# The order of SyncE's transfers in a projection's last batch, and a feed-forward stage and a long convolution put into one program

## The reference

```python
x = x + jnp.tanh(g_xattn[0]) * _L0_xattn_ref(_layernorm(x, axis=-1), ctx_2048, mask, mask, Wq, bq, Wk, bk, Wv, bv)
x = x + jnp.tanh(g_ffn[0]) * _L0_ffn_ref(_layernorm(x, axis=-1), w_gate, w_up, w_down)
x = x + jnp.tanh(g_xattn[1]) * _L1_xattn_ref(_layernorm(x, axis=-1), k, fside, ctx_2048, ctx_2048, 8)
x = x + jnp.tanh(g_ffn[1]) * _L1_ffn_ref(_layernorm(x, axis=-1), w_fc, w_proj)
```

```python
kv = vr[:, :, :, None, :] * x2r[:, :, None, :, :]      # all 64 pairs (i, j) of a group
y = causal_convolution(kv, k[group]) + kv * skip
out = jnp.einsum('bhijl,bhil->bhjl', y, x1r)
```

## Time and profile before

| | |
|---|---|
| median of 3 runs | 1246.86 us (1246.72 to 1247.12) |
| profiled execution | 1245.74 us, of which the span from the first to the last instruction is 1243.9 |
| TensorE (PE) busy | 1075.5 us, 86% |
| VectorE (DVE) busy | 997.0 us, 80% |
| ScalarE (ACT) busy | 695.9 us, 56% |
| GpSimd (POOL) busy | 514.3 us, 41% |
| mean granted TensorE clock | 0.953 of full speed |

### The profile page before, as it was taken

The page is one execution under the profiler, slowest core; times in us unless marked ns, Lnnn a source line. Parts: engine busy times, 40 slices in busy tenths (PEclk is TensorE's granted clock), DMA queues, the critical chain, the costliest instruction groups (busy, mean ns, idle before and its releaser), DMA issues. The chain is left out here.

```text
span 1243.9 us, 14018 instructions
## 1 busy us (share of the span) xinstructions
PE 1075.5 (86%) x4802; PEld 421.4 (34%) x4802; DVE 997.0 (80%) x1521; ACT 695.9 (56%) x835; POOL 514.3 (41%) x403
## 2 busy tenths in 40 slices
PE   4889689999999999778999967999999996279586
PEld 2444222222222222134444433444444443134232
DVE  4368679999999996298999955888788878677897
ACT  2777488888888888746666641110000000786996
POOL 2665323553543543611011017878887881000111
PEclk9999899999999999999999988999999997599889
DMA  9899733644644642051111110112212120000011
GB/s 325 268 380 385 241 114 104 194 128 136 192 125 135 197 123 92 28 195 51 35 52 35 52 38 29 57 52 68 68 51 68 52 67 1 0 1 1 18 51 68
DMA packets 73703, 132.89 MB, mean 107 GB/s; under 512 B 18336, under 2 KB 37152, under 8 KB 73120
## 3 DMA queue, kind: packets, MB, share of 16 engines
q1 hardware_dynamic: 73632, 132.00, 32.5%
HBM read 107.58 MB, written 22.02 MB: 104 GB/s over the span
## 5 line engine op out<-in xcount | busy, mean ns | idle before, releaser
L897 DVE TENSOR_REDUCE mneg<-ps_m 128x1 f32<-128x512 f32 x512 | 326.4, 685 | 40.0 <-PE ps_m L809 36.3
L1470 PE MATMUL ps_y<-kv,toeplitz_sb 128*128 128x512 f32 x640 | 279.1, 595 | 8.8 <-POOL kv L1382 8.8
L749 ACT ACTIVATE probs<-ps_s 128x1024 f32<-128x1024 f32 x256 | 250.7, 1022 | 37.9 <-PE ps_s L842 37.8
L1470 PEld LDWEIGHTS ps_y<-kv,toeplitz_sb 128*128 128x128 f32 x640 | 120.9, 191 | 154.8 <-issue 154.8
L842 PE MATMUL ps_s<-qk_stack 128*128 128x512 bf16 x512 | 139.6, 387 | 29.2 <-ACT probs L749 28.2
L852 PE MATMUL ps_o<-probs,v_all 128*17 128x512 f32 x1024 | 135.8, 603 | 0.0
L1382 POOL TENSOR_TENSOR kv<-vT,ctxT_sb 128x2048 f32<-128x2048 f32 x32 | 118.7, 3711 | 39.2 <-PE ps_y L1470 32.1
L1088 PE MATMUL ps_g<-w,xT_f 128*128 128x512 bf16 x512 | 119.6, 382 | 11.5 <-DVE h_f L1254 7.9
L809 PE MATMUL ps_m<-qk_stack 64*128 64x512 bf16 x512 | 112.1, 392 | 15.2 <-DVE mneg L897 8.1
L1435 ACT ACTIVATE w_anchor<-w_f 128x512 f32<-128x512 f32 x32 | 20.1, 628 | 180.6 <-DMA w_f<-in_w 180.6
L1536 DVE TENSOR_TENSOR z<-ps_y,ctxT_sb 128x1024 f32<-128x1024 f32 x64 | 77.9, 1218 | 46.8 <-PE ps_y L1470 46.8
(11 more groups left out here) (163 smaller groups left out, 1613.7 us busy)
## 6 DMA issues: line engine op xcount, KB each, us to landing
qk_stack<-qk_parts SPq DMA_DIRECT2D x192, 128.0 KB, 2.9
w_sweep<-in_w SPq DMA_DIRECT2D x8, 1536.0 KB, 11.8
qk_parts<-qk_part SPq DMA_DIRECT2D x16, 768.0 KB, 9.0
w_sweep<-in_w SPq DMA_DIRECT2D x16, 768.0 KB, 5.5
w_sweep<-in_w SPq DMA_DIRECT2D x16, 512.0 KB, 3.6
toeplitz_sb<-in_toeplitz SPq DMA_DIRECT2D x32, 256.0 KB, 2.6
w_f<-in_w SPq DMA_DIRECT2D x32, 256.0 KB, 2.9
v_rows<-vp SPq DMA_DIRECT2D x8, 544.0 KB, 10.0
```

The lines of the kernel that those rows point to most:

```text
L749: nc.scalar.activation(pr[:, k % 2, 2 * slot:2 * slot + 2, :], S[:, 2 * slot:2 * slot + 2, :], ACT.Exp).then_inc(exp_done, 1)
L897: nc.vector.tensor_reduce(mneg[:, h, tc, hd:hd + 1], M[:, bank_, :], AX.X, ALU.max, negate=True).then_inc(max_red, 1)
L1470: mm = nc.tensor.matmul(Y[:, q % 3, l2, :], T[:, g % 2, (lt - m) * P:(lt - m + 1) * P], kv[:, g % 2, m, :], start=(m == 0), stop=(m == lt))
```

## The change

Two parts.

SyncE's order. `load_constants` is split from `load_masks`. In the last batch, after the store of the key parts, SyncE now issues the weights of unit 0, then the masks and the three leading blocks of slot 2, then stores query parts and values, then everything else (other blocks and constants of slot 2, weights of unit 1, all of slot 3). The wait of `evacuate` in unit 0 is split: the even sums wait for the values of even batches, the odd ones for those of odd batches.

One program. Feed-forward and the convolution are issued in one block. Feed-forward's tiles work in the order of `ORDER`: first the 8 row blocks of channels 0-127 (t even), then the others. Their normalisation factors are made on their own: `ln_variance` in tile 9, `ln_scalar` on ScalarE in tile 9, `ln_inverse` and a shift in tile 10. ScalarE normalises the 8 row blocks in tiles 12 to 15 (`normalise_ahead`, two a tile) directly into the part of vT that is free; TensorE turns them at the end of feed-forward (`turn_in`, two before the down product of tile 14, six after it, before tile 15's hidden values are turned) and ScalarE places them. GpSimd goes on with the partition reduction and the first products after tile 14's update; tile 15's update comes after the first products. The other 8 row blocks are turned in during groups 2 to 9. Tensors of the convolution are laid over those of feed-forward, and waits guard that.

```diff
-LN_COLUMNS = ((0, ROWT), (0, ROWT - 2), (ROWT - 2, ROWT), (0, ROWT), (0, ROWT))
+LN_COLUMNS = (range(ROWT), range(ROWT - 2), range(ROWT - 2, ROWT), range(0, ROWT, CT), range(1, ROWT, CT), range(ROWT))
+ORDER = (*range(0, ROWT, CT), *range(1, ROWT, CT))
...
         if h == 0:
-            sp.wait_ge(wsum_ready, 3 * B)
-            load_unit(core, sp, 1, 0)
-        else:
             sp.wait_ge(k_done, B)
             sp.wait_ge(v_done, B)
             load_weights(sp, 0, 0)
-            sp.wait_ge(f_ready, 2 * B)
-            load_unit(core, sp, 1, 1)
+            sp.wait_ge(wsum_ready, 3 * B)
+            load_masks(core, sp, 1, 0)
+            load_blocks(core, sp, 1, 0, range(LEAD))
+        else:
+            load_blocks(core, sp, 1, 0, range(LEAD, BLOCKS))
+            load_constants(core, sp, 1, 0)
             load_weights(sp, 1, 1)
+            load_masks(core, sp, 1, 1)
+            load_blocks(core, sp, 1, 1, range(BLOCKS))
+            load_constants(core, sp, 1, 1)
...
-            if u == 0 and G == 0:
-                for p in range(2):
-                    act.wait_ge(v_stored[p], 16 * (B // 2))
+            if u == 0:
+                act.wait_ge(v_stored[G], 16 * (B // 2))
...
             if last:
+                pe.wait_ge(h_ready, NCH * ROWT - 1)
+                for i in range(2):
+                    turn_in(pe, i)
                 down(t - 1, 1 - par, False)
+                for i in range(2, ROWT // 2):
+                    turn_in(pe, i)
                 turn_h(t, par, False)
                 down(t, par, False)
...
+                if c == 3 and t == ROWT // 2 + 1:
+                    ln_scalar(core, act, 3)
+                if c in (1, 3) and t >= ROWT - 4:
+                    normalise(act, 2 * (t - ROWT + 4) + c // 2)
             if last:
+                for i in range(2):
+                    place(act, i)
                 take_down(t - 1, 1 - par, False)
+                for i in range(2, 4):
+                    place(act, i)
                 round_h(t, par)
+                for i in range(4, ROWT // 2):
+                    place(act, i)
                 copy_h(t, par)
                 take_down(t, par, False)
...
+                if c == 2 and t == ROWT // 2 + 2:
+                    ln_inverse(core, dve, 3)
+                    nc.vector.scalar_tensor_tensor(core.x_shift[:, 0:ROWT:CT], core.mean[:, 0:ROWT:CT], -1.0,
+                                                   core.rstd[:, 0:ROWT:CT], ALU.mult, ALU.mult)\
+                        .then_inc(shift_ready, 1)
...
+                if c == 3 and t == ROWT // 2 + 1:
+                    ln_variance(core, dve, 3)
...
+    def normalise_ahead(act, b):
+
+        if b == 0:
+            act.wait_ge(shift_ready, 1)
+        t = CT * b
+        nc.scalar.activation(rows(b), X[:, t, :].rearrange("p (l c) -> p l c", l=LT), ACT.Identity,
+                             bias=core.x_shift[:, t:t + 1], scale=core.rstd[:, t:t + 1]).then_inc(xe_ready, 1)
...
+    def gpsimd(pool):
+        pool.wait_ge(w8_run, ROWT)
+        nc.gpsimd.partition_all_reduce(w8s[:, MA, :], core.w8_max, P, bass.bass_isa.ReduceOp.max)\
+            .then_inc(w8_all, 1)
...
+            if g % (NGRP // 2) == 0:
+                pool.wait_ge(vT_ready, ROWT if g else HALF)
+            if g == 0:
+                pool.wait_ge(h_ready, NCH * ROWT)
...
+        for g in range(NGRP):
+            products(g)
+            gains(g)
+            if g == 0:
+                ffn_update(pool, ROWT - 1)
...
+        for g in range(NGRP):
+            pe.wait_ge(T_loaded[g % 2], 16 * (g // 2) + 16)
+            pe.wait_ge(kv_ready, g + 1)
+            if g == 1:
+                pe.wait_ge(d_taken, ROWT)
+            convolve(g, 0)
+            convolve(g, 1)
+            if 2 <= g < HALF + 2:
+                turn_in(pe, HALF + g - 2)
...
+            if g == 0:
+                ffn_statistics(dve, ROWT - 1)
+                ln_variance(core, dve, 4)
+            if g == 1:
+                ln_inverse(core, dve, 4)
```

More of the change, by code:

```diff
@@ L70, in load_masks, with load_constants @@
                          src[:, b].unsqueeze(1).to_broadcast([HD, QUAD, L])).then_inc(core.qk_lead[slot], 16)
-            if b < 2:
-                sp.dma_start(heads[SIDE * (1 - a) + LEAD:SIDE * (2 - a):STEP],
-                             src[BLOCKS:BLOCKS + 1, 0].unsqueeze(1).to_broadcast([HD, QUAD, L]))\
-                    .then_inc(core.qk_rest[slot], 16)
+def load_constants(core, sp, b, h):
+    slot = 2 * (b % 2) + h
+    for a in range(2):
+        for dst, src in ((core.Q, core.mask_q), (core.K, core.mask_k)):
+            sp.dma_start(dst[slot][SIDE * (1 - a) + LEAD:SIDE * (2 - a):STEP, QUAD * a:QUAD * (a + 1), :],
+                         src[BLOCKS:BLOCKS + 1, 0].unsqueeze(1).to_broadcast([HD, QUAD, L]))\
+                .then_inc(core.qk_rest[slot], 16)
 def load_blocks(core, sp, b, h, blocks):
@@ L101, in row_stats, with ln_columns, ln_variance @@
     core.nc.vector.bn_stats(core.bn[:, bass.ds(t, 1), :], core.X[:, bass.ds(t, 1), :]).then_inc(core.stats_step, 1)
-LN_COLUMNS = ((0, ROWT), (0, ROWT - 2), (ROWT - 2, ROWT), (0, ROWT), (0, ROWT))
-def ln_vector(core, dve, r):
-    lo, hi = LN_COLUMNS[r]
-    nc, st, tmp = core.nc, core.bn[:, lo:hi], core.ln_tmp[:, :, lo:hi]
-    n = [sum(h - l + 7 for l, h in LN_COLUMNS[0:r]) + hi - lo]
+LN_COLUMNS = (range(ROWT), range(ROWT - 2), range(ROWT - 2, ROWT), range(0, ROWT, CT), range(1, ROWT, CT), range(ROWT))
+ORDER = (*range(0, ROWT, CT), *range(1, ROWT, CT))
+def ln_columns(r):
+    cols = LN_COLUMNS[r]
+    return slice(cols.start, cols.stop, cols.step), sum(len(c) + 7 for c in LN_COLUMNS[0:r]) + len(cols)
+def ln_variance(core, dve, r):
+    cols, steps = ln_columns(r)
+    nc, st, tmp = core.nc, core.bn[:, cols], core.ln_tmp[:, :, cols]
+    n = [steps]
     dve.wait_ge(core.stats_step, n[0])
@@ L1158, in scalar, with statistics @@
         over_tiles(act, ROWT, tile)
+    def statistics(dve, t):
+        dve.wait_ge(xf_updated, t + 1)
+        dve.wait_ge(xf_start, 1)
+        row_stats(core, ORDER[t])
     def vector(dve):
@@ L1274, in tile @@
                 sweep(t, par)
-                statistics(t - 1)
-                statistics(t)
+                statistics(dve, t - 1)
         over_tiles(dve, ROWT, tile)
-    def gpsimd(pool):
-        def tile(t, par, first, last):
-            pool.wait_ge(d_taken, t + 1)
-            pool.wait_ge(xf_start, 1)
-            xt = X[:, t:t + 1, :]
-            nc.gpsimd.tensor_tensor(xt, xt, ds[:], ALU.add).then_inc(xf_updated, 1)
-        over_tiles(pool, ROWT, tile)
-    return Phase(sync, gpsimd, scalar, tensor, vector)
@@ L1948, in build @@
          vector_first) = first
-        bt = phase_bitlinear(core, ctx, A, *tail)
+        bt, rest = phase_bitlinear(core, ctx, A, *tail)
+        cv, turn_in, normalise_ahead, place = phase_longconv(core, ctx, A, rest)
         with nc.Block() as block:
```

489 lines of the change are left out of this document (243 added, 246 removed).

## The result

| | before | after |
|---|---|---|
| median | 1246.79 us (4 runs, 1246.40 to 1247.12) | 1228.87 us (4 runs, 1226.68 to 1230.88) |
| ratio | 1 | 0.986, 95% interval 0.9841 to 0.9878 |
| profiled execution, span | 1245.74, 1243.9 us | 1229.71, 1227.9 us |
| TensorE busy | 1075.5 us, 86% | 1065.7 us, 87% |
| VectorE busy | 997.0 us, 80% | 994.6 us, 81% |

The change saves 17.9 us, 1.4%; forecast were 15.8. The runs of after differ by 4.2 us from each other, those of before by 0.7.

A forecast was written before the change was run, and what follows sets the result against it. Two holes, in attention unit 0 and before the convolution; otherwise VectorE bounds feed-forward, TensorE the convolution. Terms -7.7 and -8.1 (-10.0 + 1.9) make -15.8: 1245.74 - 15.8 + 1.1 = 1231.0 us; forecast case 1228 to 1234, range 1224.5 to 1236.5.

The forecast's parts named there:

- the slow restart: Unit 1's scores after TensorE's new idle time: matmuls at the lower clock level cost 0.2 us, at most 0.9.
- the join: Feed-forward into convolution as one program: the convolution's first matmul at 745.7 instead of 755.76, gain 10.0 us.
- The first hole: Attention unit 0: ScalarE's 11.81 us wait for the ternary weights' transfer goes whole when SyncE issues it second.
- The new wait on the maximum row: Unit 1's scores: SyncE's 45-transfer backlog delays the maximum row, so they start at 166.0, not 162.1; TensorE idles 3.9 us.
- Rival A: SyncE's queue before unit 1: done in time, so part 1 gives 11.8 us and the time is 1226.9; chance 0.20.
- rival D: SyncE's backlog: every issue slows to 1.3 us, unit 1 starts 18.8 us later than before, time 1257.6; chance 0.05.
- part 1: SyncE's new order in attention: 7.9 us gained up to unit 1's scores, with the restart -7.7 us.
- The normalisation chain: VectorE in feed-forward tiles 9 and 10: seven small operations, a reciprocal and a shift add about 1.9 us.
- Rival B: Feed-forward tile 9: the chain costs 5.2 us as in tile 2, +3.3 over the 1.9, time 1234.3; chance 0.17.
- The eight normalisations in tiles 12 to 15: ScalarE in feed-forward's tail: eight of 0.80 us, two a tile, fit gaps of 1.55 and 1.07 and cost nothing.
- a bound (11): Join's upper bound: gain 11 us if feed-forward's tail does not move and a program's start was part of the first gap.
- Rival C: Feed-forward to convolution: programs not really overlapped, part 3 gives nothing, the 1.9 stay, time 1241; chance 0.08.

The follow-up runs named there:

- the earlier row: After, with the two transfers of unit 1's maximum row issued after slot 3's three leading blocks, 10 transfers sooner: 1229.74 us, ratio 0.9864.
- the kernel with one moved transfer: Before, with only the transfer of unit 0's ternary weights put right after the store of the key parts: 1242.11 us, ratio 0.9954.
- one program alone: After, with SyncE's old order put back, leaving the joined program and split statistics: 1236.68 us, ratio 0.9905.
- earlier row with the additions moved, with and without the reduction: After, maximum row earlier, weight-sum additions moved from VectorE to TensorE's matmul: 1225.06 us with GpSimd's reduction; 1215.83 us with that maximum on TensorE and VectorE instead.
- SyncE's order alone: Before, with SyncE's new order alone, three programs staying: 1241.12 us, ratio 0.9944.
- after with the old values wait: After, with unit 0's first evacuation again waiting for all stored values instead of those of the even batches: 1230.41 us, ratio 0.9857.
- maximum on TensorE: After, with the maximum over partitions found on TensorE and VectorE instead of GpSimd's reduction: 1218.87 us, ratio 0.9786.
- additions moved alone: After, with the weight-sum additions moved from VectorE to TensorE's matmul with ones, maximum row not earlier: 1226.82 us, ratio 0.9843.
- no reduction: After, with GpSimd's partition reduction replaced by an ordinary GpSimd copy, so the last layer's weight scale is wrong: 1218.81 us, ratio 0.9785.
- the two last kernels: After, maximum row earlier and maximum over partitions on TensorE and VectorE: ratio 0.9751 (1212.68 to 1217.49 us); the same with additions off VectorE: 1215.83 us, ratio 0.9753.

## Why the prediction was right

The time, 1228.87 us, lies in the forecast's own range, 2.1 us under the value. Its mechanism held step by step, but that the sum came out so near is in part luck: the two misses of size among its terms, +1.8 for the slow restart and -2.05 for the join, cancel. By the profiled executions the gain is 16.0 us against 15.8. The 2.1 us are nearly all the step from the profiled execution to the median: I added 1.1, since before's profiled execution lay that much under its median, and after's lies 0.8 over its own.

**The first hole, -11.8.** As forecast: rounding at 145.9, no wait, the weights second in SyncE's queue where they were behind the stores.

**The new wait on the maximum row, +3.9.** As forecast, in place, cause and size. From the store of the key parts to unit 1's scores I had 166.0 - 131.5 = 34.5 us; it is 34.3. The wait is 3.73. That it is SyncE's backlog is shown by the earlier row, which takes it away, and by the kernel with one moved transfer, which has it. (The row's transfers are 8 KB each, not the 32 KB by which I took their landing; from the end of the backlog to unit 1's scores it is 2.6 us, 2.7 in the forecast.) Rival A (SyncE done in time) and rival D (issues at 1.3 us) are out: the 45 transfers took 31.7 us, 0.70 each.

**The slow restart, +0.2 (at most 0.9).** Mis-sized: 2.0. I had compared unit 0 of before with the unit after it, where the hole lay inside unit 0. Now it lies at the start of unit 1, and there a slow TensorE is on the path; that the place makes the difference is my reading, no run moved the hole. For it speaks that from the first exponential to the written row unit 0 of before took 26.51 us, less the hole of 11.81 the same 14.70 as after's, which has no hole: there the slow restart cost nothing. The traces line up, but for 0.1 us, by idle time before unit 1's scores; from there to its first rounding:

| kernel | TensorE idle | us to the rounding |
|---|---|---|
| before; one program alone; earlier row; earlier row with the additions moved, with and without the reduction | 0 | 5.60 |
| SyncE's order alone | 1.56 | 5.62 |
| after with the old values wait; maximum on TensorE | 2.73 | 7.06, 7.07 |
| additions moved alone | 2.77 | 7.18 |
| no reduction | 3.59 | 7.64 |
| after | 3.73 | 7.64 |
| weights alone | 4.13 | 7.54 |

So part 1 gave 6.1 us in the trace instead of 7.7; the slow restart is 1.8 of it, and the shorter way to unit 1's scores gave 0.2 back.

**The normalisation chain, +1.9.** Measured +1.78: tile 9 takes 647.02 - 633.54 = 13.48 us, tile 10 12.34, all others of the second half 12.03. Rival B (5.2) is out. VectorE's first instruction of tiles 9 and 10:

```profile
633.54 0.15 DVE L1286 COPY sc_f<-sc_f 128x1 f32<-128x1 f32 x1
647.02 0.14 DVE L1286 COPY sc_f<-sc_f 128x1 f32<-128x1 f32 x1
```

The eight normalisations in tiles 12 to 15 cost nothing, as reckoned.

**The join, -10.0.** Mis-sized: -12.05. The chain update, gap, reduction, gap, product, matmul is as forecast. Three of its links were long: I allowed 0.3 us for the turns ahead of tile 14's update, and there are none (721.48 is 14.0 us after tile 15's start, as in before); the first gap is 5.57 and not 7.0; the second 6.90 and not 7.12. The 7.0 had been read from a program's start to the reduction, so by the difference some 1.4 us of it were the start of a program, which the change removes. I had this as a bound (11) and not as the value, and the bound was itself 1 us short. In six kernels with the joined program the first gap is 5.5 to 5.8 us, the second 6.9 to 7.2. Rival C (no overlap) is out.

**What no step covered.** The store of the key parts came 1.26 us later and feed-forward's first five tiles took 1.1 less. I take both for chance: over the twelve traces that store lies between 131.4 and 134.4 us, 134.4 in the kernel with only the weights moved, which is before itself up to there, and the five tiles take between 71.6 and 73.9.

**The Trainium skill** (GPSIMD Engine Reference, 2.1 Instruction dispatch) gives about 6 us for the first call to freshly loaded code. The gap on the way in, 5.57, agrees with it. The one on the way back, 6.90, it doesn't name, and it is as real: with the operation taken away both are gone. What fills the gaps isn't shown. I read them as loading of code; between 729 and 736 in after, inside the second gap, the trace has no DMA packet at all, so it doesn't bear that reading out.

**Open** is what spreads the runs of after over 4.2 us. With four or five executions of a kernel, and with 1.7 to 5.6 us for before from chip to chip, the spreads tell little across the batches. The clean pair are the two last kernels, on one chip: 4.8 us with the additions, 1.6 without, at about the same median.

## What to carry to other kernels

A queue that works in order has a backlog, and a stall elsewhere hides it: before taking a stall away, sum up the queue's issues to see who waits for its end next, and place the small transfer that is wanted first ahead of the many that are not. Here one custom operation on GpSimd had 12 us of gaps around its 0.4; if nothing long is left beside it, do it on other engines. A wait that remains also absorbs the variation ahead of it, so the gain of removing it is not its length in one profile.

## What the runs showed of the hardware

- The reduction over partitions on GpSimd takes 0.37 us and has 5.5 to 5.8 us without a releaser ahead of it and 6.9 to 7.2 behind it; a second call at once costs nothing measurable, and without it both gaps are gone (10.0 us of the kernel's time, 8.5 of them in the way to the convolution's first matmul; the first 60 matmuls, without idle time ahead of them, took 1.8 less).
- Some small operations of VectorE on SBUF ended only with the GpSimd operation beside them: two additions of 128x3 took 3.13 us instead of 0.42. In the kernel with the maximum on TensorE a scaling of two columns, with one input, did so too beside the product of 726.24 to 729.95, while the reciprocal just ahead of it did not:

```profile
726.91 0.17 DVE L1616 RECIPROCAL w_s<-columns 128x2 f32<-128x2 f32 x1
727.11 2.86 DVE L1618 TENSOR_SCALAR w_s<-w_s 128x2 f32<-128x2 f32 x1
```

- After 1.56 us of idle TensorE four score matmuls still took 1.04 us; after 2.73 and more they took 1.89, and the unit lost 1.5 to 2.0 us.
